# Row statistics of the FFN taken in the attention stage, and four places of the FFN stage's DVE and ACT order moved

## The reference

```python
h = tokens(x); h = concatenate([h, text(x_txt)], axis=1)
h = h + attention(layernorm(h))
h = h + ffn(layernorm(h))

def bitlinear(x, w, g):                    # ffn: bitlinear(gelu(bitlinear(x, w1, g1)), w2, g2)
    xn = x * rsqrt(mean(x * x) + 1e-6) * g
    scale = 127.0 / clip(max(abs(xn)), 1e-5)
    xq = clip(round(xn * scale), -128, 127) / scale
    return einsum('bsd,fd->bsf', xq, weight_quant(w))
```

## Time and profile before

| | |
|---|---|
| median of 3 runs | 1758.22 us (1755.66 to 1758.87) |
| profiled execution, its own time | 1756.77 us |
| its span, first to last instruction | 1755.0 us |
| busy over the span | PE 84%, DVE 83%, ACT 70%, POOL 63% |
| mean granted PE clock | 0.91 of 2.4 GHz |

### The profile page before, as it was taken

The page is one execution under the profiler, slowest core; times in us unless marked ns, Lnnn a source line. Parts: engine busy times, 40 slices in busy tenths (PEclk is TensorE's granted clock), DMA queues, the critical chain, the costliest instruction groups (busy, mean ns, idle before and its releaser), DMA issues.

```text
span 1755.0 us, 53767 instructions
## 1 busy us (share of the span) xinstructions
PE 1474.0 (84%) x18602; PEld 1203.9 (69%) x18602; DVE 1460.8 (83%) x3227; ACT 1232.5 (70%) x1862; POOL 1099.7 (63%) x1369
## 2 busy tenths in 40 slices
PE   4799999999999999999999999985555565656565
PEld 2678888888888888888888888874444454545454
DVE  5578888888888888888888888864899999999996
ACT  0466676767667676767667676752788888888887
POOL 5456566666666665656665656541777777777775
PEclk8899999999999999999999999996677878777876
DMA  8533434333434342434343333310000000000000
GB/s 204 81 60 61 67 60 68 60 68 60 68 58 69 56 71 54 73 53 74 53 72 56 71 56 70 58 56 18 9 24 20 24 20 24 20 24 20 24 20 29
DMA packets 104194, 93.57 MB, mean 53 GB/s; under 512 B 22737, under 2 KB 94466, under 8 KB 104162
## 3 DMA queue, kind: packets, MB, share of 16 engines
q1 hardware_dynamic: 103394, 91.58, 27.5%
q0 software_dynamic: 768, 1.57, 0.4%
HBM read 74.12 MB, written 11.91 MB: 49 GB/s over the span
## 4 chain that ended last, share of the span: by engine, by line
PE 65%; DVE 19%; issue 7%; ACT 3%; POOL 1%; DMA 1%; DVEq 1%; SPq 1%; ACTq 0%; POOLq 0%
PE ps L1038 19%; PE ps L1095 9%; PE ps L1181 8%; DVE nmax L677 6%; PE ps L1172 5%; PE ps L1128 5%; DVE ff_st L814 4%; PE ps L1280 3%; PE ps L1160 3%; PE ps L1154 3%; PE ps L1261 3%; PE ps L1133 2%; PE ps L1076 2%; PE ps L1109 2%; DVE xpix L807 1%
## 5 line engine op out<-in xcount | busy, mean ns | idle before, releaser
L1038 PE MATMUL ps<-w_eff,pix 124*112 124x193 f32 (+1 forms) x2048 | 406.8, 337 | 11.6 <-DMA pix<-side 9.2
L677 DVE TENSOR_REDUCE nmax<-ps 116x12 bf16<-116x1344 f32 (+2 forms) x192 | 302.9, 1578 | 88.4 <-PE ps L1133 87.8
L493 POOL TENSOR_TENSOR pix<-probs,g_b 112x192 f32<-112x192 f32 (+1 forms) x512 | 298.4, 613 | 104.7 <-ACT probs L993 95.4
L881 ACT ACTIVATE probs<-ps,isw 116x688 f32<-116x688 f32 x384 | 299.1, 831 | 85.4 <-PE ps L1160 83.1
L1038 PEld LDWEIGHTS ps<-w_eff,pix 124*112 124x112 f32 (+1 forms) x2048 | 308.1, 166 | 38.3 <-issue 23.3
L420 POOL TENSOR_TENSOR xsq<-xsq 124x784 f32<-124x784 f32 (+1 forms) x128 | 184.3, 1440 | 218.1 <-ACT xsq L874 213.1
L440 POOL TENSOR_SCALAR_AFFINE_SELECT probs<-probs 116x464 f32<-116x464 f32 x384 | 274.1, 726 | 68.0 <-ACT probs L881 59.5
L863 ACT ACTIVATE pix<-xpix 54x896 f32<-54x896 f32 (+1 forms) x128 | 196.6, 1538 | 1.9 <-DMA xpix<-in_x 1.1
L1250 PE MATMUL ps<-ident_h,xpix 112*96 112x112 f16 (+1 forms) x256 | 34.9, 281 | 186.4 <-DVE xpix L831 186.4
L1095 PE MATMUL ps<-xnT,wq_pad 97*128 97x228 f32 (+1 forms) x768 | 166.5, 366 | 0.0
L1250 PEld LDWEIGHTS ps<-ident_h,xpix 112*96 112x96 f16 (+1 forms) x256 | 23.8, 167 | 197.8 <-DVE xpix L831 102.5
(11 more groups left out here) (134 smaller groups left out, 3230.9 us busy)
## 6 DMA issues: line engine op xcount, KB each, us to landing
xpix<-in_x SPq DMA_DIRECT2D x192, 196.0 KB
rden<-den_rows SPq DMA_DIRECT2D x256, 85.5 KB, 2.2
out<-xpix SPq DMA_DIRECT2D x64, 87.0 KB
out<-xpix SPq DMA_DIRECT2D x64, 84.0 KB
xpix<-in_x SPq DMA_DIRECT2D x128, 34.1 KB
h_all<-shift_w SPq DMA_DIRECT2D x5, 768.0 KB, 4.4
pix<-side SPq DMA_DIRECT2D x64, 36.8 KB
pix<-side SPq DMA_DIRECT2D x64, 36.6 KB
```

The lines of the kernel that those rows point to most:

```text
L493: last = nc.gpsimd.tensor_tensor(v2[0:P, b, tile, cols], gel[0:P, b, tile, cols], g2_b[0:P, cols], ALU.mult)
L677: V.tensor_reduce(dst, src, AX_X, ALU.max, negate=True).then_inc(s_mx, 1)
L881: A(probs[0:TB, g, 2 * e:2 * e + 2, :], ps[0:TB, 4 + 2 * e:6 + 2 * e, 0:SK], ACT.Exp, scale=isw[0:TB, 7:8]).then_inc(s_p, 1)
L1038: last = MM(ps_tok[tile][0:P, :], pix[0:HI, par, o, lo:lo + P], w_eff[0:HI, o, :], start=(o == 0), stop=(o == OFFS - 1))
```

## The change

`bn_stats` and `bn_aggr` of the final rows move from the FFN's DVE step to a new function `measure_rows`, called in the attention step between the first and the second maxima of the next image; means are kept for all images in `mean2`. Their roots are made on POOL by the new `row_roots`, behind `patch_roots`, and kept in `roots`. FFN's POOL step makes only the roots of Gelu's mean square (128x2 in place of 128x4). In the FFN step of DVE, the mean square of Gelu's output comes after `v1` and its maxima, the final addition comes after the maxima of `v2`, and the product of scale and weight step comes last, behind the first quantisation, with a semaphore of its own (`f_step`) for Gelu. In the FFN step of ACT the squares come ahead of the `q2T` copy. PE's program stays as it is.

```diff
+            def row_roots(m):                      # POOL
+                pool.wait_ge(s_agg2, m + 1)
+                after(pool, s_rms, m)
+                apart(pool)
+                nc.gpsimd.tensor_scalar(ln_st[:, 32:34], ln_st[:, 35:38:2], 1.0 + EPS_RMS, EPS_LN * EPS_RMS,
+                                        ALU.mult, ALU.add).then_inc(s_var2, 1)
+                pool.wait_ge(s_var2, m + 1)
+                nc.gpsimd.tensor_tensor(roots[:, bass.ds(m * 4, 2)], ln_st[:, 32:34], expo[:, 0:2],
+                                        ALU.pow).then_inc(s_rms, 1)
...
                 if newer:
                     patch_roots(n + 2)
+                if prev:
+                    row_roots(n - 2)
...
+            def measure_rows(n):                   # DVE
+                dve.wait_ge(s_h2, n + 1)
+                apart(dve)
+                for tile, P in enumerate((TA, TB)):
+                    last = V.bn_stats(ln_st[0:P, 20 + 6 * tile:26 + 6 * tile], h_all[0:P, hcols(n, tile)])
+                last.then_inc(s_rowst, 1)
+                dve.wait_ge(s_rowst, n + 1)
+                after(dve, s_var2, n)
+                apart(dve)
+                for tile, P in enumerate((TA, TB)):
+                    last = V.bn_aggr(ln_st[0:P, 34 + 2 * tile:36 + 2 * tile], ln_st[0:P, 20 + 6 * tile:26 + 6 * tile])
+                last.then_inc(s_agg2, 1)
+                dve.wait_ge(s_agg2, n + 1)
+                V.tensor_copy(mean2[:, bass.ds(n * 2, 2)], ln_st[:, 34:38:2]).then_inc(s_mean2, 1)
...
                 if new:
                     maxima(n + 1, 0)
+                if prev:
+                    measure_rows(n - 1)
+                if new:
                     maxima(n + 1, 1)
```

More of the change, by code:

```diff
@@ L42 @@
 EPS_LN, EPS_RMS = 1e-5, 1e-6
-LIMIT, ROWB, TEXT, V_SETUP = 19, 26, 29, 33
+LIMIT, ROWB, TEXT, V_SETUP = 21, 28, 31, 35
 EARLY = 4
@@ L475, in _, with ffn_step @@
             step_images(IMAGES - 1, 0, None, newer=False, newest=False)
[L477 to L481, removed]
+            row_roots(IMAGES - 2)
+            row_roots(IMAGES - 1)
+            def ffn_step(i, b, mid=True):
+                if mid:
+                    pool.wait_ge(f_var, i)
+                    nc.gpsimd.tensor_tensor(roots[:, bass.ds(i * 4 + 6, 2)], ff_st[:, b, 18:20], expo[:, 0:2],
                                             ALU.pow).then_inc(f_r1, 1)
@@ L506, in _ @@
             ffn_step(IMAGES - 2, 0)
-            ffn_step(IMAGES - 1, 1, new=False)
-            ffn_step(IMAGES, 0, new=False)
+            ffn_step(IMAGES - 1, 1)
+            ffn_step(IMAGES, 0)
         @block.vector
@@ L527, in _ @@
             step(V.memset(ff_st[:, :, :], 1.0))
+            step(V.memset(mean2[:, :], 1.0))
+            step(V.memset(roots[:, :], 1.0))
             step(V.memset(gel_sum[:, :, :], 1.0))
@@ L774, in ffn_step @@
                 if new:
[L775 to L793, removed]
+                    after(dve, f_q1, m)
                     for tile, P in enumerate((TA, TB)):
                         ins = V.scalar_tensor_tensor(v1[0:P, tile, :], h_all[0:P, hcols(m, tile)],
-                                                     st[0:P, 12 + 2 * tile:13 + 2 * tile], g1_b[0:P, :],
+                                                     mean2[0:P, bass.ds(m * 2 + tile, 1)], g1_b[0:P, :],
                                                      ALU.subtract, ALU.mult)
@@ L801, in ffn_step @@
                                               apply_absolute_value=True)
+                if mid:
+                    dve.wait_ge(f_ssq, 2 * j + 2)
+                    V.tensor_scalar(st[:, 18:20], gel_sum[:, 1 - b, :], 1.0 / HIDDEN, EPS_RMS, ALU.mult,
+                                    ALU.add).then_inc(f_var, 1)
+                if mid:
+                    dve.wait_ge(f_v2, 2 * j + 2)
+                    for tile, P in enumerate((TA, TB)):
+                        ins = V.tensor_reduce(st[0:P, 26 + tile:27 + tile], v2[0:P, 1 - b, tile, :], AX_X,
+                                              ALU.max, apply_absolute_value=True)
+                if new or mid:
+                    flinks[0] += 1
+                    ins.then_inc(f_vc, 1)
                 if last_:
@@ L995, in ffn_step @@
                           scale=ff_st[0:P, b, 40 + tile:41 + tile]).then_inc(f_g, 1)
+                if new:
+                    after(act, f_var, m - 1)
+                    for tile, P in enumerate((TA, TB)):
+                        act.wait_ge(f_g, 2 * m + tile + 1)
+                        A(gsq[0:P, tile, :], gel[0:P, 1 - b, tile, :], ACT.Square,
+                          accum_out=gel_sum[0:P, 1 - b, tile:tile + 1]).then_inc(f_ssq, 1)
                 if mid:
@@ L1002, in ffn_step @@
                     ins.then_inc(f_t2s, 1)
[L1003 to L1008, removed]
             act.wait_ge(s_h2, IMAGES)
```

48 lines of the change are left out of this document (28 added, 20 removed).

## The result

The change makes the kernel slower: 1796.98 us (median of 4 runs, 1793.41 to 1799.83) against 1758.06 us, a ratio of 1.0223, 95% interval 1.0210 to 1.0236. The profiled execution took 1793.41 us, its span 1791.7 us: 36.7 us more than the 1755.0 of before.

A forecast was written before the change was run, and what follows sets the result against it. Attention was tied to DVE's second maxima without slack, the FFN to DVE's order (7.97 us). Span 1755.0 + 20.5 + 0.7 + 14.1 = 1790.3, plus 1.8 around it and 1.4 to the median: 1793.5 us, range 1738 to 1818.

The forecast's parts named there:

- Row statistics: DVE in attention: `measure_rows` delays the second maxima and PE's next score round, 0.33 us a step, +20.5 us.
- `row_roots`: POOL in attention: the new roots take 1.25 us, within PE's slack of 0.2 us, so cost 0.
- DVE's own floor: DVE in the FFN step: removed statistics lower its floor from 7.97 to about 6.5 us; it stops being the bound.
- The loop: FFN, ACT and PE: the `q2T` copy behind Gelu and squares closes a loop of 8.59 us at low clock.
- Four low turns in five: FFN: PE's clock is low in four turns of five, mean period 8.2 us, +14.1 us over 60 steps.
- the high clock holds: Rival, FFN: PE stays at 2.4 GHz in nearly every step, period 6.8 us, 1709 us; chance 0.20.
- attention hides the statistics: Rival, attention: DVE's 0.80 us idle and PE's patches absorb the statistics, only the FFN term stays, 1773 us; chance 0.07.
- That rival's 1820 us: Rival, POOL late in attention: PE's second L1172 group waits up to 0.5 us a step, +31 us; chance 0.08.

The follow-up runs named there:

- E5: Changed kernel with the row statistics split: the two BN_STATS ahead of the first maxima, BN_AGGR and the copy behind them; 1772.74 us.
- E6: Changed kernel with ACT's squares back behind the `q2T` copy and 12 idle matmuls a step in the FFN; 1722.97 us.
- E4: Changed kernel with 12 idle matmuls, results unread, added behind `turn_second` in every FFN step; 1730.11 us.
- E1: Changed kernel with ACT's squares put back behind the `q2T` copy, all else as changed; 1743.99 us.
- E2: Kernel before with one edit, ACT's squares moved ahead of the `q2T` copy; 1791.02 us.
- E11: Changed kernel with the squares back behind the `q2T` copy and the statistics split over two waits, without idle matmuls; 1720.91 us.
- E7: Changed kernel with the squares back, the statistics split over two waits and 12 idle matmuls a step; 1699.31 us.
- E12: E6 with POOL weighting only a quarter of each probability tile's columns, the rest left out; 1703.17 us.
- E10: E7 with 6 idle matmuls a step in place of 12; 1708.45 us.

## Why the prediction was right

The forecast of 1793.5 us stands 0.2% under the 1796.98 measured, and both mechanisms, the statistics ahead of the second maxima and the loop through the copy, are shown by runs. That the number is so close is in part luck: the even FFN steps cost 12.8 us and not 14.1, the forecast had nothing for the 3.6 us at the end, and the ground on which it chose its share of low turns does not hold. The span came out 1.4 us above the forecast's 1790.3; the other 2 us are that the profiled execution was the fastest of the four. By its steps:

- *Row statistics, +20.5 us (0.33 us a step), and +0.7 us at the end of attention.* Measured +0.34 us a step and 1.08 us of wait for the last roots. The first `v1` of all comes 21.94 us later (1251.10 against 1229.16), against the 21.2 of the forecast; at the first of the 60 steps it is 20.25, as the first FFN steps have lost L777 to L785. The working was 0.13 us short of the length (1.29 us from 616.88 to 618.17, not 1.16: the copy also waits for its own aggregate), and the second maxima come 0.41 us later, of which the period shows 0.34. E5 shows the cause: spread over two waits, the same instructions cost nothing.
- *`row_roots`, 1.25 us, cost 0.* They take 1.66 us (608.47 to 610.13), above my upper bound of 1.5, by which PE should have been late. It was not, because the L458 behind them became shorter: four in 2.26 us, 0.57 each, where two took 1.81 us. In the kernel before they ran beside DVE's addition to `h_all` (its timeline):

```profile
617.45 1.43 DVE L638 SCALAR_TENSOR_TENSOR h_all<-tok_t,front_st,bw 112x192 f32 x2
```

  That took 1.43 us, and the same two instructions (L662) take 0.73 us in the change. The cost of 0 was right by luck, through a gain that I had not seen; that gain also gave DVE most of the 0.68 us of idle time which E5 used. No run takes `row_roots` away, so that POOL and DVE now pass each other because of them is read from the order in the traces and not tested.
- *DVE's own floor, 6.5 us.* Wrong: E6, where DVE has next to no waits, needs 7.07 us, 6.85 of it busy. The rows subtracted were right, but the rest does not keep its length when it moves: in the new order `v1`, with two SBUF inputs, stands beside POOL's weighting (1.15 us for two in place of 0.73), and the weight step too. Which of the moves on DVE puts `v1` there was not tested apart. The forecast did not rest on this number, since the loop was longer. It did mislead the expectation of E4, and in part that of E1.
- *The loop, 8.59 us at the low clock.* Measured 8.70 in the turn shown, the same members in the same order. The largest difference is from the copy's end to L1316: 0.14 us (1605.33 to 1605.47), where the forecast had 0.05, for which it gave no row. E1 opens it by the move alone (7.395 us), E2 makes it by the move alone (8.484 us), E4 shortens its PE part by the clock alone (7.224 us).
- *Four low turns in five, 8.2 us, +14.1 us.* Measured 8.182 us, +12.8 us. By the extremes 6.6 and 8.70, three quarters are low; but few turns are wholly high, half are mixed. The ground for the choice fails. I took the level from how long PE had been idle, and in this kernel that does not tell it:

```profile
1292.24 1.19 PE L1316 MATMUL ps<-w2t,xpix 128*112 128x192 f16 x12 [2.75 <-ACT xpix L1043]
...
1308.08 2.16 PE L1316 MATMUL ps<-w2t,xpix 128*112 128x192 f16 x12 [2.22 <-ACT xpix L1043]
```

  With the waits of 0.45 and 0.67 us ahead of the four transposes before them, the first was high after 3.20 us of idle time and the second low after 2.89. Of the turns from 1275 to 1780 us, 7 had L1316 high after 2.38 to 3.19 us, 41 had it low after 2.51 to 3.68, and 14 ran partly at each level. The working had a slip too: half of a low turn's 5.84 us of PE work is 2.9 us and not 3.4, which leaves 3.7 us idle; the trace has 3.68 behind such a turn (up to 1299.02). So the choice of four in five was lucky.
- *Not forecast: 3.6 us at the end.* The last steps run through the loop as well: from one L1316 to the next are 8.15 us (1768.61 to 1776.76) near the end.
- *The rivals.* That the high clock holds did not happen (0.72 against 0.78); E4 shows that it would have made the change a gain of 1.4%. That attention hides the statistics fails on the 1.29 us against the 0.80; E5 is what makes it true. POOL's two new instructions took longer than I priced, without effect: PE waited 0.9 us in total for L458. That rival's 1820 us was added up wrong, too: 1793.5 and 31 are 1824.5.

Put together: on the FFN step DVE's edits bring -0.57 us (before to E1), the squares' new place +0.79 us (E1 to changed), the statistics +0.34 us on the attention step. A gain of some 34 us was there; the move of two squares took 47 us over 60 steps.

## What to carry to other kernels

Before an instruction is moved ahead of a copy, follow what the copy releases round to the instruction: if it comes back to the same engine within a step, the moved time is added to a loop, and no engine's busy share shows it. Work put into a wait is free only up to the length of that wait; two short waits can take what one cannot. When the bound of a step goes through matmuls and PE otherwise waits, look at the granted clock: unread matmuls in the gap bought 22 us here even in the best order (E11 to E7).

## What the runs showed of the hardware

- DVE instructions with two SBUF inputs wait for the piece of POOL's weighting in progress. The same weight step L866 of the changed kernel, beside the weighting and, in the last steps, without it (timeline of DVE):

```profile
1766.45 0.55 DVE L866 TENSOR_TENSOR ff_st<-ff_st,w_step 128x4 f32<-128x4 f32 x1
```
```profile
1772.45 0.15 DVE L866 TENSOR_TENSOR ff_st<-ff_st,w_step 128x4 f32<-128x4 f32 x1
```

  The Trainium skill (SBUF — State Buffer, SBUF: two separate sides) calls the pair of ports that VectorE and GpSimd share an exclusive lock for the whole instruction. The trace agrees, to 0.02 us in the row of E12 above. Over the FFN step three quarters of the weighting are worth 1.2 us of DVE's busy time (6.85 in E6, 5.66 in E12), and the profile counts that waiting as busy.
- Two SBUF inputs are not the whole condition. The tensor-scalar L853 has one tensor input and is long beside the weighting too (E6, then E12, 1290 to 1690 us), while the final addition L844, whose other input lies in PSUM, takes 408 ns in both:

```profile
L853 DVE TENSOR_SCALAR ff_st<-ff_st 128x4 f32<-128x4 f32 x56 | 28.2, 504 | 1.9
```
```profile
L853 DVE TENSOR_SCALAR ff_st<-ff_st 128x4 f32<-128x4 f32 x59 | 10.1, 170 | 2.0
```

- It works both ways. In the changed kernel (1290 to 1690 us) a piece of POOL's weighting takes 0.79 us on average beside `v1` (120 pieces) and 0.61 us elsewhere (269 pieces). Two affine selects took 1.81 us beside DVE's `h_all` addition, and four took 2.26 us behind it.
- Adding 12 matmuls a step that nobody reads raised the granted clock of the stage from 0.72 to 0.92 and took 67 us off the changed kernel. The Trainium skill (TensorE: Matmul & The Clock Gate, Why this matters for your kernels) warns of idle gaps between bursts; E10 shows that half the filling gives the clock about half way (0.82).
